# Attention in a decoder layer on one core: three job banks and one bank for the sums, sums in two chunks a group, first scores over 40 slots

## The reference, cut to what matters

```python
q, k, v = heads(x @ Wq + bq), heads(x @ Wk + bk), heads(x @ Wv + bv)     # 16 heads of 16
att = einsum('bhqd,bhkd->bhqk', q, k) * scale                            # 512 x 512, causal
y = einsum('bhqk,bhkd->bhqd', softmax(att), v)
qc, kc, vc = ...                                                         # keys, values from a context of 64
y = y + einsum('bhqk,bhkd->bhqd', softmax(qc kc^T * scale), vc)
x = layernorm(x + y @ Wp + bp)
```

## Time and profile before

| | us |
|---|---|
| median of 3 runs | 2476.27 |
| lowest and highest | 2471.98, 2476.95 |
| the profiled execution, its own time | 2472.55 |
| its span, first to last instruction | 2470.5 |
| attention steps of the batches 0 to 14, each | about 77 |
| mean granted clock of PE over the span, share of full | 0.941 |

### The profile page before, as it was taken

One profiled execution on the slowest core, in us unless ns is written; L12 is line 12 of the kernel. 1 busy time (PEld: TensorE's weight loads), 2 busy tenths in 40 slices (PEclk: granted clock), 3 DMA queues, 4 the chain that ended last, 5 costly groups with the idle time before them and its releaser, 6 DMA issues. The chain is left out here.

```text
span 2470.5 us, 43737 instructions
## 1 busy us (share of the span) xinstructions
PE 2109.8 (85%) x13056; PEld 1445.7 (59%) x13056; DVE 1622.0 (66%) x2908; ACT 1083.7 (44%) x2100; POOL 855.9 (35%) x1260
## 2 busy tenths in 40 slices
PE   6775968898898885799998998999989899974998
PEld 4554857777777774455555555555555556532554
DVE  7897445555555552777776786767867678733776
ACT  4453223223232321355555554555545555552554
POOL 3232624434344442133333333333333333331222
PEclk9998979999999996999999999999999999996999
DMA  3333011111111114334244242433424424201222
GB/s 103 125 122 120 23 68 35 61 67 58 53 59 68 43 60 103 75 74 104 68 86 93 80 95 70 84 93 73 102 64 90 93 73 103 44 18 63 85 85 68
DMA packets 104522, 188.35 MB, mean 76 GB/s; under 512 B 27800, under 2 KB 77848, under 8 KB 98184
## 3 DMA queue, kind: packets, MB, share of 16 engines
q1 hardware_dynamic: 104328, 185.97, 27.9%
HBM read 110.07 MB, written 58.79 MB: 68 GB/s over the span
## 5 line engine op out<-in xcount | busy, mean ns | idle before, releaser
L1589 DVE TENSOR_REDUCE at_mneg<-at_ps_s 128x1 f32<-128x384 f32 (+3 forms) x704 | 436.9, 636 | 93.0 <-PE at_ps_s L1253 91.0
L1378 ACT ACTIVATE at_pt<-at_ps_w 128x512 f32<-128x512 f32 x640 | 373.8, 597 | 266.0 <-PE at_ps_w L1264 261.6
L1459 POOL TENSOR_SCALAR_AFFINE_SELECT at_pt<-at_pt 128x256 f32<-128x256 f32 (+1 forms) x640 | 232.1, 367 | 586.2 <-ACT at_pt L1378 581.6
L1252 PE MATMUL at_ps_s<-at_ks,at_qs 96*128 96x128 bf16 (+3 forms) x1024 | 263.9, 310 | 21.3 <-DMA at_ks<-parts_d 12.5
L1264 PE MATMUL at_ps_w<-at_qs,at_ks 97*128 97x512 bf16 (+3 forms) x1024 | 245.8, 302 | 20.2 <-issue 16.6
L1252 PEld LDWEIGHTS at_ps_s<-at_ks,at_qs 96*128 96x128 bf16 x1024 | 85.3, 100 | 213.0 <-issue 98.8
L796 POOL TENSOR_TENSOR ml_m_lo<-ml_m,ml_m_hi 112x512 fp32r<-112x512 f32 x96 | 125.9, 1319 | 234.4 <-ACT ml_m_hi L732 234.4
L1279 PE MATMUL at_ps_o<-at_pt,at_val 128*32 128x512 f32 (+3 forms) x2048 | 177.6, 442 | 4.2 <-POOL at_pt L1459 4.1
L1253 PE MATMUL at_ps_s<-at_mask,at_ident 128*128 128x128 bf16 (+2 forms) x704 | 174.5, 248 | 0.0
L1415 POOL TENSOR_TENSOR at_parts<-at_rest,at_parts 128x512 bf16<-128x512 f32 x64 | 75.0, 1171 | 211.1 <-ACT at_parts L1364 211.1
L743 ACT ACTIVATE ml_gl<-ml_ps_g 112x512 f32<-112x512 f32 x96 | 55.3, 591 | 204.9 <-PE ml_ps_u L125 204.9
(11 more groups left out here) (234 smaller groups left out, 5712.4 us busy)
## 6 DMA issues: line engine op xcount, KB each, us to landing
parts_d<-at_parts SPq DMA_DIRECT2D x64, 384.0 KB, 2.5
at_ks<-parts_d SPq DMA_DIRECT2D x192, 128.0 KB, 7.6
at_qs<-parts_d SPq DMA_DIRECT2D x32, 384.0 KB, 5.5
pj_xin<-in_x SPq DMA_DIRECT2D x16, 512.0 KB, 4.3
gate_d<-pj_zc SPq DMA_DIRECT2D x16, 512.0 KB, 2.6
xv_all<-pj_turned_xv SPq DMA_DIRECT2D x16, 512.0 KB, 3.3
ml_turned_y<-xv_all SPq DMA_DIRECT2D x16, 512.0 KB, 3.3
ml_x<-gate_d SPq DMA_DIRECT2D x16, 512.0 KB, 4.2
```

Source lines behind the costliest of these rows:

```text
L1252: pe.matmul(out[:, i, :], qs[par][0:ROWS, h, toks], ks[par][0:ROWS, h, 0:(qt + 1) * P], start=i == 0, stop=False)
L1378: act.activation(pt[u % RING][:], ps_w[u % 2][:], ACT.Exp, scale=SCALE).then_inc(exped, 1)
L1459: pool.affine_select(out=diag, in_=diag, compare_op=ALU.is_ge, fill=0.0, base=0, pattern=pattern, channel_multiplier=-1).then_inc(cut, 1)
L1589: dve.tensor_reduce(mneg[:, g, h0 % HG:h0 % HG + count, qt], view_score(ps_s[s % 2], qt, count), AX_X, ALU.max, negate=True).then_inc(maxe ...
```

## The change

The banks go from 2 + 2 + 2 + 2 to 3 for jobs, 1 for the sums, 2 and 2. A job's bank is then that of the job three positions earlier. The sums of key tiles 1, 3 and 2 become one chunk, issued where the last of them stood (slot 11 of a group instead of slots 9 and 11, counted from the group's first). With one bank `ps_o`, the first chunk of a group waits for DVE's division of the group before (`y_set`). `turn_out` and `divide` stand one slot after the copy instead of two, and the 44 first scores stand in slots 0 to 39 instead of 0 to 41: slots 0, 10, 20 and 30 hold two, where before slots 0 and 21 did. DVE waits for its own earlier r job before it writes `rdenc` again.

```diff
-CHUNKS = [(g, c) for g in range(NG) for c in range(3)]
+CHUNKS = [(g, c) for g in range(NG) for c in range(2)]
-CHUNK_OF = [CHUNKS.index((g, c)) for g, c, _ in UNITS]
+CHUNK_OF = [CHUNKS.index((g, min(c, 1))) for g, c, _ in UNITS]
...
-BANK = {j: p % 2 for p, j in enumerate(JOBS)}
+BANKS = 3
+BANK = {j: p % BANKS for p, j in enumerate(JOBS)}
...
-SCORED_IN = [[s for s in range(NS) if s * (len(SLOTS) - 2) // NS == u] for u in range(len(SLOTS))]
+SCORED_IN = [[s for s in range(NS) if s * (len(SLOTS) - 4) // NS == u] for u in range(len(SLOTS))]
...
-        ps_j = [n.psum(f"ps_j{i}", [P, 512]) for i in range(2)]
-        ps_o = [n.psum(f"ps_o{i}", [P, 512]) for i in range(2)]
+        ps_j = [n.psum(f"ps_j{i}", [P, 512]) for i in range(BANKS)]
+        ps_o = n.psum("ps_o", [P, 512])
...
             def outputs(b, par, k):
                 pe.wait_ge(cut, NU * b + LAST_UNIT[k] + 1)
                 if c == 0:
-                    wait(pe, y_set, NG * b + g - 1)
+                    wait(pe, y_set, NG * b + g)
...
-                for kt in ((0,), (1, 3), (2,))[c]:
+                for kt in ((0,), (1, 3, 2))[c]:
...
-                    if back(b) and u - 2 * LAG in LAST_UNIT[2::3]:
-                        turn_out(b, LAST_UNIT[2::3].index(u - 2 * LAG))
+                    if back(b) and u - LAG - 1 in LAST_UNIT[1::2]:
+                        turn_out(b, LAST_UNIT[1::2].index(u - LAG - 1))
...
+                    wait(dve, *(clear(f"r{i - 1}", b) if i else clear("r3", b - 1)))
                     dve.reciprocal(rdenc[:], src[:, :, :, HD]).then_inc(rdenc_set, 1)
```

More of the change, by code:

```diff
@@ L978 @@
 MEMBERS = {"lead": LEAD, "front": FRONT, "tail": TAIL}
-ON_BANK = {kind: [[j for j in jobs if BANK[j] == i] for i in range(2)] for kind, jobs in MEMBERS.items()}
-SCORED_IN = [[s for s in range(NS) if s * (len(SLOTS) - 2) // NS == u] for u in range(len(SLOTS))]
+ON_BANK = {kind: [[j for j in jobs if BANK[j] == i] for i in range(BANKS)] for kind, jobs in MEMBERS.items()}
+SCORED_IN = [[s for s in range(NS) if s * (len(SLOTS) - 4) // NS == u] for u in range(len(SLOTS))]
 HALF = NU // 2
@@ L1035, in attend @@
         ready = {kind: n.sem(f"{kind}_ready") for kind in MEMBERS}
-        cleared_on = {kind: [n.sem(f"{kind}_clear{i}") for i in range(2)] for kind in MEMBERS}
+        cleared_on = {kind: [n.sem(f"{kind}_clear{i}") for i in range(BANKS)] for kind in MEMBERS}
         front_ready, tail_ready, lead_ready = ready["front"], ready["tail"], ready["lead"]
@@ L1173, in cleared @@
             def cleared(names, name, b):
-                others = [j for j in names if BANK[j] != BANK[name]]
-                if others:
-                    pe.wait_ge(*clear(others[-1], b))
+                for i in range(BANKS):
+                    own = [j for j in names if BANK[j] == i]
+                    if own:
+                        pe.wait_ge(*clear(own[-1], b))
             def job(name, b, npar):
@@ L1366, in copy_out @@
             def copy_out(b, g):
-                act.wait_ge(summed, NCH * b + 3 * (g + 1))
+                act.wait_ge(summed, NCH * b + 2 * (g + 1))
                 wait(act, out_turned, NG * b + g)
-                act.activation(so[:], ps_o[g % 2][:], ACT.Copy).then_inc(out_copied, 1)
+                act.activation(so[:], ps_o[:], ACT.Copy).then_inc(out_copied, 1)
             def step(b, par):
@@ L1383, in step @@
                             middle(name, b + 2)
-                    if back(b) and u - LAG in LAST_UNIT[2::3]:
-                        copy_out(b, LAST_UNIT[2::3].index(u - LAG))
+                    if back(b) and u - LAG in LAST_UNIT[1::2]:
+                        copy_out(b, LAST_UNIT[1::2].index(u - LAG))
             over_steps(act, step)
```

15 lines of the change are left out of this document (8 added, 7 removed).

## The result

| | before | after |
|---|---|---|
| median, us | 2476.2 | 2503.9 |
| lowest and highest of 4 runs | 2472.0, 2477.0 | 2497.4, 2506.7 |
| span of the profiled execution | 2470.5 | 2500.4 |
| mean granted clock of PE | 0.941 | 0.942 |

The changed kernel is slower: ratio 1.0112, 95% interval 1.0088 to 1.0135, that is 27.7 us. The forecast was 2515, range 2474 to 2534. The sign of the change and the places of the new waits came as forecast, but for one at w0; the loss was forecast at 39 us and measured at 28.

A forecast was written before the change was run, and what follows sets the result against it. PE, the busiest engine, sets a step by its work plus stalls, many on DVE. Net 2.6 us a step over fifteen steps (39 us) plus 3 for the last batch, on 2472.55, gave 2515 us, range 2474 to 2534.

The forecast's parts named there:

- The old stalls go, 4.4 us a step: PE's waits at q1, k1, v0 and n3 vanish, with smaller gaps: 4.4 us a step; q0's wait stays.
- Slots 9 to 20, 3.35 us: New PE waits a step: 0.85 us in slot 10, 0.35 at w0, 1.35 and 0.8 in slot 20.
- Slots 30 to 32, 2.2 us: New PE waits a step: 0.5 and 1.45 us at slot 30's two scores, 0.3 at slot 32's turn.
- The end, 1.75 us: Step's end, new waits: 0.45 us at slot 34's score, 0.5 at slot 41's last sums, 0.8 at `turn_out`.
- The sum: Per step, new waits 7.3 us less old 4.4, net 2.9; carried through slot by slot 2.4; taken as 2.6.
- the sentence that the change alters no work: Whole step: same matmuls, copies and reduces in another order, so only PE's stalls change; no size for work.
- The last batch: Last batch, without scores: a group's sums follow the cut of its last tile, partly hidden, 3 us more.
- The sign "78 to 80 us a step": In the new profile, a step of 78 to 80 us would show the forecast right.
- The rule on banks: Skill's advice to rotate matmul groups through PSUM banks; alone, job stalls go and nothing comes; speaks against two scores a slot.
- Faster (2428): Rival: scores find their reduces done, old 3.2 us a step go and little comes: 2428 us; chance 0.13.
- A chain on the single sums bank: Rival: `ps_o` chains sums, copy, turn and division, clock falls twice: 4 us a step, 2536 us and more; chance 0.1.
- The clock: PE's granted clock over the steps: no change taken, bounds 0.7 us a step either way, 10 us in all.

The follow-up runs named there:

- experiment 5: The changed kernel with first scores back over 42 slots and sums in three chunks a group again: 2452.2 us, 20.6 below the kernel before.
- experiment 1: The changed kernel with only the first scores put back over 42 slots: 2442.2 us, 30.1 below the kernel before.
- experiment 8: The changed kernel with scores over 42 slots, layernorm spread over slots 21 to 24 and turn two slots behind the copy: 2417.9 us.
- experiment 6: The changed kernel with DVE's layernorm taken out of slot 18 and spread over slots 21 to 24: 2487.1 us, 14.3 above the kernel before.
- experiment 3: The changed kernel with sums in three chunks a group again, scores still over 40 slots: 2471.1 us, 1.2 below the kernel before.
- experiment 2: The kernel before with only its first scores placed over 40 slots: 2486.6 us, 14.3 above the kernel before.
- experiment 4: The changed kernel with the third bank given to the first scores instead of the jobs: 2472.9 us, 0.5 above the kernel before.

## Why the prediction came out as it did

The forecast got the sign and, but for one at w0 that did not come and a small one in slot 8 that did, the places and sizes of the new waits. Its loss was too large by 11 us, mainly because the term for what goes was too small, and the lead-in was left out. To compare its waits with the trace one has to measure as it did: from the moment when PE could have started the next matmul. The brackets start at the drawn end, about 0.15 us later. In slot 10, say, the mask ahead starts at 1363.29 in the changed kernel, the next matmul could have started 0.22 later, and it starts at 1364.35: 0.84 us, where the bracket has 0.68.

- **The old stalls go, 4.4 us a step.** Right in every place: the waits at q1, k1, v0 and n3 are gone, q0's stays. Experiment 5 gives what banks and early turn are worth without the rest: 17.1 us in its fifteen steps, 1.1 a step and not 4.4, since waits for row maxima take over part of it there too (25.2 us of them between 1110 and 2200 of its trace), and a turn waits 0.78. The 0.93 of n3 had two reasons to go; experiment 1 shows that the early turn alone hides it, and experiment 8 that it returns without that.
- **Slots 9 to 20, 3.35 us.** Forecast 0.85 in slot 10, 0.35 at w0, 1.35 and 0.8 in slot 20; measured 0.84, none, 1.35 and 0.80, in all 3.0. The w0 wait is the step that failed: s3's subtraction ends at 1379.33, and the weights ahead of w0 leave PE free only at 1379.44. The reason given for slot 20, the layernorm, is only part of it: taken away, k1's half and DVE's wait for ACT hold the same reduce (experiment 6).
- **Slots 30 to 32, 2.2 us.** Forecast 0.5 and 1.45 in slot 30 and 0.3 at the turn in slot 32; measured 0.71, 1.47 and 0.30, in all 2.5.
- **The end, 1.75 us.** Forecast 0.45, 0.5 and 0.8; measured 0.46, 0.59 and 0.87, in all 1.9.
- **The sum.** The new waits are 7.4 us a step, where the forecast had 7.3, besides 0.18 in slot 8 that I had not foreseen. A step grew by 2.13, not 2.6, so what went is about 5.4 and not 4.4: this is the term that was mis-sized. Most of the missing 1.0 was put at nothing by the sentence that the change alters no work. The sums that were two pieces took 1.00 and 0.57 us and take 1.43 as one block, and one gap of 0.1 ahead of a piece has gone (the block of slot 31 starts 0.33 behind the product ahead of it, 1403.96 to 1404.29, where a score starts 0.23 behind one, 1361.62 to 1361.85). For four groups that is about 1 us a step; PE's busy time is 9.3 us less in fifteen steps, which agrees in sign and roughly in size. The 31.9 us of the fifteen steps stand against 39.
- **The last batch.** It gave 2.9, forecast 3, but the agreement is partly luck: it ran at a granted clock of 0.95, and at 1.00 before. Experiment 1, with the same two chunks, took 36.2 at 0.95; experiment 3, with three, 34.3 at 1.00. How much of the 2.9 is the clock is not shown.
- **The lead-in was left out.** I had counted steps from batch 0 on only. From the attention's first instruction to the first weights it took 98.3 us before and takes 92.4. The waits for a full job bank are fewer there, as in the steps: 8.8 us for `at_rest` and `at_sd` before, 2.6 after. But the waits for row maxima rose from 4.7 to 9.5 and the one for the first keys from 12.5 to 14.9, so the waits that the trace names are only some 2 us fewer; the rest is busy time of PE, 65.0 and 61.1, and its cause stays open. The stretch takes 98.3 and 99.5 us in the two kernels with the old banks (before, experiment 2), 96.1 with three score banks (experiment 4), and 90.9 to 95.1 in the ten traces with three job banks, so it goes with the banks. 31.9 + 2.9 - 6.5 + 1.6 = 29.9 of the profiled span.
- **The sign "78 to 80 us a step".** The mean step is 77.8, just outside; it started from 75.6 and not from 77.
- **The rule on banks.** The third job bank takes away the stalls it should, and 42 slots let the gain through. Optimizing Tensor Performance, Matmuls (the Trainium skill, Perfetto Trace Analysis) says to rotate independent matmul groups over banks so that emptying one overlaps filling the next; the runs agree, for jobs (experiment 5) and for scores (experiment 4) alike.
- **The rivals.** Faster (2428) needed new waits under 4.4 us; they were 7.4. Its mechanism is real though: with the placing of before it comes to 2442 (experiment 1). A chain on the single sums bank as the cause of a larger loss is excluded: in experiments 1 and 5 it stands and the kernel is faster than before; no wait of the first sums for `y_set` appears. No run prices the extra semaphore waits apart, which the forecast took as nothing.
- **The clock.** 0.942 beside 0.941 over the span and 0.98 in both over the fifteen steps, no change, as taken.

So the 27.7 us are made of: banks and early turn -20.6, scores over 40 slots +19.4, two chunks -9.5, and +38.4 that only scores and chunks together cost (57.8 - 19.4), since the sums had been the cover of the slots that now hold two scores. Over the fifteen steps alone the same parts are -17.1, +21.2, -13.2 and +41.1, in all 31.9. The forecast had this joint term in its slots 10 and 30 (the sums that left slots 9 and 29), and did not see that without it the rest would be a gain.

## What to carry to other kernels

A buffer bank more can move a wait to the next resource that the same reader empties, as it did here; before adding it, list what that reader must do, in its own order, ahead of each release, and whether two producers now meet between releases. Edits that share a slack are not additive: one line cost 14, 19 or 58 us, and joining the sums into fewer chunks was worth -9.5 or +28.9, by what else was in place, so take such a change apart before you keep or drop it whole. An in-order engine that idles in a trace is spare only if nothing of what you want from it stands behind what it waits for.

## What the runs showed of the hardware

A large block of sums is denser than its parts: 24 small matmuls took 1.43 us from their start to the next score (1404.29 to 1405.72), where the 16 and 8 of before took 1.00 and 0.57 in the same measure.

The idle time called issue at the loop's return differed between kernels with nothing changed there, and less within one: 3.1 to 3.5 us before, 3.2 to 3.7 in the changed kernel, 4.5 to 4.8 in experiment 3 and 3.1 to 3.8 in experiment 8, five returns each; it was not followed up.
